# Probabilities in fp16 halves turned by DMA, row sums divided after the product with v, and another order within a slot

## What is computed

```python
h = shift_token(x); q, k, v = split(h @ wqkv)            # 8 heads of 64
q, k = rotary_xpos(l2norm(q) * qs, l2norm(k) * ksc)
attn = softmax(mask(8 * q @ k.T))                         # windows of 128 rows see 256 columns
x = x + (attn @ v) @ wo
h = layernorm(shift_token(x)) * lg + lb
a, g = split(h @ w1 + b1); x = x + (a * gelu(g)) @ w2 + b2
```

## Time and profile before

| | us |
|---|---|
| median of 3 runs (3177.46 to 3179.95) | 3179.91 |
| the profiled execution, its time | 3178.97 |
| its span, first to last instruction | 3177.2 |
| first attention and setup, to the first transfer of the slots | 774 |
| slots, two layers | 774 to 3177 |

### The profile page before, as it was taken

One profiled execution on the slowest core, in us unless ns is written; L12 is line 12 of the kernel. 1 busy time (PEld: TensorE's weight loads), 2 busy tenths in 40 slices (PEclk: granted clock), 3 DMA queues, 4 the chain that ended last, 5 costly groups with the idle time before them and its releaser, 6 DMA issues.

```text
span 3177.2 us, 79721 instructions
## 1 busy us (share of the span) xinstructions
PE 2982.5 (94%) x24952; PEld 2581.8 (81%) x24952; DVE 2656.8 (84%) x7754; ACT 1847.9 (58%) x4226; POOL 1754.4 (55%) x2083
## 2 busy tenths in 40 slices
PE   6898989783899999999999999999999999999997
PEld 3676767573688888888888888888888888888886
DVE  6878788755788888888888888899998999999895
ACT  4233241402566666666666666666676676676673
POOL 1231314024566666666666666676676676676773
PEclk9999999995899999999999999999999999999999
DMA  1120202025111111111111111222112212122221
GB/s 38 38 70 28 80 14 87 4 83 205 33 50 49 53 51 49 52 48 49 54 50 50 50 48 50 56 56 60 56 55 57 65 55 60 55 55 60 63 56 46
DMA packets 273326, 177.65 MB, mean 56 GB/s; under 512 B 95758, under 2 KB 271090, under 8 KB 272754
## 3 DMA queue, kind: packets, MB, share of 16 engines
q1 hardware_dynamic: 273138, 175.50, 19.0%
HBM read 104.08 MB, written 54.54 MB: 50 GB/s over the span
## 4 chain that ended last, share of the span: by engine, by line
PE 72%; POOL 1%; issue 1%; DVE 0%; DMA 0%; ACT 0%; POOLq 0%; SPq 0%; DVEq 0%; ACTq 0%
PE b_ps L824 17%; PE b_ps L899 14%; PE b_ps L910 10%; PE b_ps L852 8%; PE b_ps L840 7%; PE b_ps L878 6%; PE b_ps L865 6%; PE b_ps L809 2%; PE b_ps L802 2%; PE b_ps L791 1%; POOL b_sq L1145 0%; POOL b_rn L1178 0%; POOL b_t L1167 0%; POOL b_kr L1183 0%; DVE b_probs L1093 0%
## 5 line engine op out<-in xcount | busy, mean ns | idle before, releaser
L957 ACT ACTIVATE b_probs<-b_probs,b_negmax 128x256 f32<-128x256 f32 x1024 | 506.0, 496 | 78.3 <-DVE b_negmax L1093 77.5
L824 PE MATMUL b_ps<-b_wqkv,b_hT_hi 128*128 128x512 f32 x1536 | 493.0, 402 | 1.0 <-DVE b_hT_lo L981 1.0
L899 PE MATMUL b_ps<-b_h2T,b_w 128*128 128x256 f16 x4224 | 473.0, 273 | 6.5 <-DMA b_h2T<-b_xh_hl 6.4
L899 PEld LDWEIGHTS b_ps<-b_h2T,b_w 128*128 128x128 f16 x4224 | 413.6, 98 | 55.1 <-DMA b_h2T<-b_xh_hl 6.8
L1145 POOL TENSOR_TENSOR b_sq<-b_sq 128x512 f32<-128x512 f32 (+5 forms) x768 | 419.3, 546 | 62.4 <-ACT b_sq L938 22.3
L1178 POOL TENSOR_TENSOR b_rn<-b_ss_min,b_mhalf 128x16 f32<-128x16 f32 x128 | 377.2, 2947 | 108.9 <-DVE b_ss_min L1005 108.7
L1106 DVE TENSOR_SCALAR b_probs<-b_probs,b_rinv 128x256 f32<-128x256 f32 x1024 | 409.6, 442 | 18.2
L1155 POOL TENSOR_TENSOR b_rstd<-b_var,b_mhalf 128x1 f32<-128x1 f32 x128 | 72.2, 564 | 552.3 <-DVE b_var L1066 552.3
L407 PE MATMUL a_ps<-a_xn_hl,a_E 128*128 128x256 f16 x3072 | 352.5, 277 | 18.9 <-DVE a_E L290 18.9
L407 PEld LDWEIGHTS a_ps<-a_xn_hl,a_E 128*128 128x128 f16 x3072 | 303.3, 99 | 58.5 <-issue 19.9
L910 PE MATMUL b_ps<-b_w,b_hid 128*128 128x256 f32 x1536 | 342.2, 379 | 1.2 <-DVE b_hid L1129 1.2
(11 more groups left out here) (137 smaller groups left out, 6191.6 us busy)
## 6 DMA issues: line engine op xcount, KB each, us to landing
b_hx<-xs_dram SPq DMA_DIRECT2D x256, 64.0 KB, 1.9
b_rot<-rot_dram SPq DMA_DIRECT2D x128, 128.0 KB, 2.1
b_xr<-xs_dram SPq DMA_DIRECT2D x128, 128.0 KB, 2.1
xp_dram<-b_xp SPq DMA_DIRECT2D x128, 128.0 KB, 1.7
b_h<-xp_dram SPq DMA_DIRECT2D x256, 64.0 KB, 1.8
a_x_res<-in_L_attn_x_dram SPq DMA_DIRECT2D x64, 128.0 KB, 2.2
x_dram<-a_x SPq DMA_DIRECT2D x64, 128.0 KB, 1.7
xs_dram<-a_xo SPq DMA_DIRECT2D x64, 128.0 KB, 1.8
```

The costliest lines, as they stand in the source:

```text
L824: last = nc.tensor.matmul(ps[:, bank, :], hT[:, k, :], wqkv[:, ds(layer(s), 1), part, k, bank * INNER:(bank + 1) * INNER], start=(k == 0 a ...
L899: last = nc.tensor.matmul(ps[:, bank, half * 2 * P:(half + 1) * 2 * P], w1[:, ds(layer(2 * j), 1), wp, k, first:first + P], h2T[:, hp, k, ...
L957: nc.scalar.activation(probs[:, h, :], probs[:, h, :], ACT.Exp, bias=negmax[:, h:h + 1], scale=-1.0, accum_out=rowsum[:, h:h + 1]).then_in ...
```

## The change

- **Probabilities.** They stay unnormalised, with a constant `P_SHIFT` added to the exponent's bias (`shift_exponent`, four small DVE operations). ACT casts each pair of heads to an fp16 high half (`high_probs`), DVE (pairs 0, 1) and POOL (pairs 2, 3) make the low half, and SP turns each pair, 128 x 1024 fp16, into `probsT` by DMA (`turn_probs`). The 16 PE transposes of a slot, their copies out of PSUM and `normalise` go.
- **Row sums.** One reciprocal of all 8 sums; 8 fp32 products with the identity (`spread_done`, bank 3) spread it over the rows of each head; ACT copies that to `spread`; DVE multiplies it with the result of the product with v into `o_n`, from which the halves of oT are made.
- **fp16.** q, k, v come from scaled fp16 halves of hT and wqkv, v is kept as two fp16 halves (`v_hl`, made by ACT and DVE), and its product takes three fp16 passes (48 products of 128 columns). The scales come from the largest weight (setup: two reductions, an all-reduce and small steps) and, for layer 1, from the largest output of layer 0 (`layer_top` on DVE in odd slots, `batch_scales` in two slots). wqkv is loaded first in the setup.
- **b2** is a row of w2, so POOL's xb goes; ACT casts xh instead of DVE.
- **Order.** PE: q, k turned; q; k; scores; v; spread; first product chunks 0, 1 (odd slots) or half of the second product (even slots); product with v; chunks 2, 3 or the other half; hx; wo; chunks 4, 5. The feed-forward products change parity. The other engines follow, as the diff shows.

The diff, cut to its core (indentation of up to 16 blanks taken off):

```diff
-W1_BANKS = (0, 1, 6, 3, 4, 5)
+W1_BANKS = (0, 1, 6, 4, 5, 3)
+SPREAD_BANK, W2_BANK = 3, 4
+SCALE_SLOTS = (NW - 4, NW + 6)
...
+def batch_scales(nc, dve, step, before, work, top, w_scale, w_unit, h_scale, o_unit, ss_floor):
+floor, pow2, inv, root = (work[:, n:n + 1] for n in range(4))
+columns = list(h_scale.shape)
+wait(dve, step, before)
+nc.vector.tensor_scalar(floor, top, H_FLOOR, None, ALU.max).then_inc(step, 1)
+dve.wait_ge(step, before + 1)
+nc.vector.tensor_scalar(pow2.bitcast(I32), floor.bitcast(I32), 0x7F800000, None, ALU.bitwise_and).then_inc(step, 1)
+dve.wait_ge(step, before + 2)
+nc.vector.reciprocal(inv, pow2).then_inc(step, 1)
+dve.wait_ge(step, before + 3)
+nc.vector.tensor_scalar(h_scale, inv.to_broadcast(columns), H_TOP, None, ALU.mult).then_inc(step, 1)
+nc.vector.tensor_scalar(root, inv, H_TOP * NORM_FLOOR, w_scale, ALU.mult, ALU.mult).then_inc(step, 1)
+dve.wait_ge(step, before + 5)
+nc.vector.tensor_tensor(ss_floor, root.to_broadcast(columns), root.to_broadcast(columns), ALU.mult).then_inc(step, 1)
+nc.vector.tensor_scalar(o_unit, pow2.to_broadcast(columns), 1.0 / (H_TOP * V_SCALE), w_unit, ALU.mult, ALU.mult).then_inc(step, 1)
...
+sp.dma_start(wqkv_f[:].rearrange("p l k n -> p (l k) n"), w["wqkv"].rearrange("l (k p) n -> p (l k) n", p=P)).then_inc(loaded_qkv, 16)
...
+dve.wait_ge(loaded_qkv, 16)
+for l in range(LAYERS):
+    nc.vector.tensor_reduce(top_q[:, l:l + 1], wqkv_f[:, l].rearrange("p k n -> p (k n)"), AX.X, ALU.max, apply_absolute_value=True).then_inc(top_q_ready, 1)
+dve.wait_ge(top_q_shared, 1)
...
-v = sb("v", [P, 4, INNER])
+hT_hi, hT_lo = sb("hT_hi", [P, KD, P], F16), sb("hT_lo", [P, KD, P], F16)
+v_hl = sb("v_hl", [P, SLOTS, 2, INNER], F16)
...
+    def turn_probs(p):
+        t = s - 1
+        if in_range(t):
+            if p < 2:
+                wait_apart(sp, p_lo_dve, 2 * t + p + 1, passed_sp)
+            else:
+                wait_apart(sp, p_lo_pool, 2 * t + p - 1, passed_sp)
+            wait_apart(sp, pv_done, t, passed_sp)
+            sp.dma_start_transpose(probsT[:, p], probs_hl[:, p].rearrange("p a n -> p (a n)")).then_inc(pT_loaded[p], 16)
...
+    turn_probs(0)
+    turn_probs(1)
     t = s - 2
     if in_range(t):
         n = stream_block(t)
         sp.wait_ge(xp_ready, t + 1)
-        sp.dma_start(xp_v[:, ds(n, 1), :], xp[:, r % 2, :]).then_inc(xp_stored, 16)
+        sp.dma_start(xp_v[:, ds(n, 1), :], xp[:, (r - 2) % SLOTS, :]).then_inc(xp_stored, 16)
+    turn_probs(2)
+    turn_probs(3)
+    if in_range(t):
         wait_apart(sp, xp_stored, 16 * (t + 1), passed_sp)
         wait_apart(sp, xh_ready, t - 1, passed_sp)
         wait(sp, h2_loaded, 32 * t)
         sp.dma_start(h2[:, r % 2, 0:HALF], xp_v[:, ds(n, 1), 0:HALF]).then_inc(h2_loaded, 16)
         sp.dma_start(h2[:, r % 2, HALF:D], xp_prev[:, ds(n - 1, 1), HALF:D]).then_inc(h2_loaded, 16)
+    t = s - 3
+    if in_range(t):
+        wait_apart(sp, xh_lo, t + 1, passed_sp)
+        wait_apart(sp, w1_done, HC * (pairs - 2 if r % 2 == 1 else pairs - 3), passed_sp)
+        wait_apart(sp, h2T_loaded, 16 * t, passed_sp)
+        n, pair = (r - 3) % 2, (r - 3) // 2 % 2
+        sp.dma_start_transpose(h2T[:, pair, :, :, n * P:(n + 1) * P].rearrange("p a k n -> p (a k) n"),
+                               xh_hl[:].rearrange("p a d -> p (a d)")).then_inc(h2T_loaded, 16)
...
+    wait(pe, o_ready, t - 2)
...
-        pe.wait_ge(v_kept, t + 1)
         wait(pe, xp_ready, s - 2)
+        if not in_range(s - 3):
+            pe.wait_ge(v_lo, s)
         for p in range(HP):
             last = nc.tensor.transpose(ps[:, 2, p * P:(p + 1) * P], qr[:, p * P:(p + 1) * P], ident_f[:])
         last.then_inc(qT_done, 1)
         pe.wait_ge(kr_ready, t + 1)
         wait(pe, scores_kept, HEADS * t)
-        if r % 2 == 1:
-            wait(pe, hid_ready, HC * (pairs - 2) + W1_BANKS.index(6) + 1)
+        if r % 2 == 0:
+            wait(pe, hid_ready, HC * (pairs - 3) + W1_BANKS.index(6) + 1)
...
+        wait(pe, q_terms, 3 * s)
         if r % 2 == 0:
-            wait(pe, xpp_ready, s - 4)
-        else:
-            wait(pe, hid_ready, HC * (pairs - 1))
-        for p in range(HP):
-            if p == HP - 1 and in_range(s - 1):
-                pe.wait_ge(kT_lo, s)
-            pe.wait_ge(probs_ready, HEADS * t + 2 * p + 2)
-            for n in range(4):
-                last = nc.tensor.transpose(ps[:, 3 + p, n * P:(n + 1) * P],
-                                           probs[:, 2 * p + n // 2, (n % 2) * P:(n % 2 + 1) * P], ident_f[:])
-            last.then_inc(pT_done, 1)
-        pe.wait_ge(v_kept, t + 1)
-        if not in_range(s):
-            pe.wait_ge(oT_lo, t)
-        for p in range(HP):
-            pe.wait_ge(pT_kept, HP * t + p + 1)
-            for c in range(2):
-                window = (r - 2 - (r + c) % 2) % 4
-                for h in range(2):
-                    last = nc.tensor.matmul(ps[h * DH:(h + 1) * DH, 7, p * P:(p + 1) * P],
-                                            v[:, window, (2 * p + h) * DH:(2 * p + h + 1) * DH],
-                                            probsT[:, p, (2 * h + c) * P:(2 * h + c + 1) * P],
-                                            start=(c == 0), stop=(c == 1))
-        last.then_inc(pv_done, 1)
+            wait(pe, hid_ready, HC * (pairs - 3) + 1)
+        qkv(0, q_done)
+        wait(pe, k_terms, 3 * s)
+        if r % 2 == 0:
+            wait(pe, hid_ready, HC * (pairs - 3) + 2)
...
+        if r % 2 == 1:
+            wait(pe, xpp_ready, s - 5)
+        else:
+            wait(pe, hid_ready, HC * (pairs - 2))
...
+    if in_range(s):
+        wait(pe, qT_lo, s)
+        qkv(2, v_done)
     t = s - 2
+    if in_range(t):
+        pe.wait_ge(rinv_ready, t + 1)
+        if in_range(s - 1):
+            pe.wait_ge(scores_kept, HEADS * (s - 1) + BANK_READ[SPREAD_BANK])
+        elif r % 2 == 0:
+            pe.wait_ge(hid_ready, HC * (pairs - 2))
+        for p in range(HP):
+            for h, rows in enumerate(half_rows):
+                last = nc.tensor.matmul(ps[rows, SPREAD_BANK, p * P:(p + 1) * P], rinv[:, 2 * p + h:2 * p + h + 1].to_broadcast([P, DH]),
+                                        ident_f[:], start=True, stop=True)
+        last.then_inc(spread_done, 1)
+    first_product((0, 1))
+    second_product(0)
+    if in_range(t):
+        pe.wait_ge(v_lo, t + 1)
+        if not in_range(s):
+            pe.wait_ge(o_ready, t)
+        for p in range(HP):
+            pe.wait_ge(pT_loaded[p], 16 * (t + 1))
+            for c in range(2):
+                window = (r - 2 - (r + c) % 2) % 4
+                for a, (vp, pp) in enumerate(PARTS):
+                    for h in range(2):
+                        last = nc.tensor.matmul(ps[h * DH:(h + 1) * DH, 7, p * P:(p + 1) * P],
+                                                v_hl[:, window, vp, (2 * p + h) * DH:(2 * p + h + 1) * DH],
+                                                probsT[:, p, 4 * pp + 2 * h + c, :],
+                                                start=(c == 0 and a == 0), stop=(c == 1 and a == 2))
+        last.then_inc(pv_done, 1)
...
+    first_product((2, 3))
+    second_product(1)
+    if in_range(s + 1):
+        transpose_hx(s + 1, r + 1)
...
+    first_product((4, 5))
...
+    def exp_pair(p):
+        t = s - 1
+        if in_range(t):
+            if p == 0:
+                wait(act, rinv_ready, t)
+            act.wait_ge(shift_done, HP * t + p + 1)
+            for h in range(2 * p, 2 * p + 2):
+                nc.scalar.activation(probs[:, h, :], probs[:, h, :], ACT.Exp, bias=negmax[:, h:h + 1], scale=-1.0,
+                                     accum_out=rowsum[:, h:h + 1]).then_inc(exp_done, 1)
+    def high_probs(p):
+        t = s - 1
+        if in_range(t):
+            act.wait_ge(exp_done, HEADS * t + 2 * p + 2)
+            wait(act, pT_loaded[p], 16 * t)
+            nc.scalar.copy(probs_hl[:, p, 0, :], probs[:, 2 * p:2 * p + 2, :].rearrange("p h n -> p (h n)")).then_inc(p_hi, 1)
...
+    exp_pair(0)
+    if in_range(s):
         act.wait_ge(v_done, s + 1)
         wait(act, pv_done, s - 2)
-        nc.scalar.copy(v[:, r, :], ps[:, 2, :]).then_inc(v_kept, 1)
+        nc.scalar.activation(v_hl[:, r, 0, :], ps[:, 2, :], ACT.Copy, scale=V_SCALE).then_inc(v_hi, 1)
+    exp_pair(1)
     t = s - 2
     if in_range(t):
-        wait(act, pv_done, t)
-        for p in range(HP):
-            act.wait_ge(pT_done, HP * t + p + 1)
-            nc.scalar.copy(probsT[:, p, :], ps[:, 3 + p, :]).then_inc(pT_kept, 1)
-        act.wait_ge(pv_done, t + 1)
+        act.wait_ge(spread_done, t + 1)
+        wait(act, o_ready, t)
+        nc.scalar.copy(spread[:], by_pair(ps[:, SPREAD_BANK, :])).then_inc(spread_kept, 1)
+    high_probs(0)
+    if in_range(t):
+        act.wait_ge(o_ready, t + 1)
         wait(act, wo_done, t)
-        nc.scalar.copy(oT[:, 0], by_pair(ps[:, 7, :])).then_inc(oT_hi, 1)
-    t = s - 1
-    if in_range(t):
-        for p in range(HP):
```

(66 more changed lines are left out.)

331 lines of the change are left out of this document (175 added, 156 removed).

## The result

The changed kernel takes 3755.38 us (median of 4 runs, 3748.59 to 3756.22), the kernel before 3179.28 on the same chip: ratio 1.181, interval 1.179 to 1.183. It is slower by 576 us, where 286 were forecast, and lies 115 us above the range. The span is 3754.0 us, the mean granted clock 0.918 (0.976 before).

The account below looks back on a forecast made before the run. PE bounds the kernel before; after the change, PE held up by chains through ACT and DVE: pair 34.7 + 6.45 = 41.1 us, +4.5. 3179 + 276 + 10 (setup) = 3465 us, range 3300 to 3640.

Parts of the forecast that it names:

- The paths: Queues of ACT and DVE after the product with v make PE wait in four places, 6.45 us a pair.
- Turning of q behind xp: After an even slot, the next slot's turning of q waits for DVE's xp (bank 2); PE stands 2.7 us.
- Turning of k behind the hidden chunks: After an odd slot, k's turning waits for the third hidden chunk, scores start late; PE stands 2.4 us.
- Spreading behind the masking: Spread products wait until DVE has masked three heads: 0.95 us in one slot, 0.4 us in the other.
- PE's own work: PE's products and turnings without waits: 0.94 us less a slot, 34.7 us a pair.
- the lower end: Product with v if halves of the array overlap: 28 ns a product, 1.33 us; the forecast took the middle, 2.0.
- The spreading: New on PE: 8 fp32 products spreading the reciprocals, 0.95 us more a slot.
- the clock falls: Rival: a tenth of the pair at 1.2 GHz, +4 us a pair, 3700 us; chance 0.06.
- The sum: Work 34.7 plus waits 6.45 gives 41.1 us a pair, +4.5 on before; times 61, +276 us.
- the setup: Reductions, all-reduce, small operations and wqkv's earlier load before the slots: 0 to 25 us more, taken as 10.
- The transposes by DMA: On SP: 2.1 us to issue each, 3.3 to land; hidden behind PE's slot and waits, so costing nothing.
- PE stays without gaps: Rival: ACT's and DVE's queues short enough, pair 34.7 us, 3075 us; chance 0.15.

Follow-up runs that it names:

- The moves against the first and against both: Changed kernel with xp right after xh on DVE, 3593.3 us; with two exponentials and a cast ahead of oT's copy on ACT, 3583.8; together 3576.8.
- spreading behind: Against the kernel with the loop's edge moved (3350.0 us): spread products behind the product with v, second layer's output norm behind the last hidden chunk; 3347.3 us.
- other banks: Changed kernel with the xp and exponential moves, plus k turned in bank 7, q in bank 6 in odd slots, hT halves made earlier; 3616.9 us.
- gelus cut: Against the kernel with other banks: gelus and hidden chunks 2 on moved behind the next slot's copies of q and k; 3587.5 us, ratio 1.128.

## Why the prediction was right and wrong

- **The paths** (right). Turning of q behind xp in the odd slot: 2.7 us forecast, 2.8 measured, and 0.4 in the even slot, which the forecast did not have. Turning of k behind the hidden chunks: 2.4, where the scores were to follow; measured 2.7 and 0.5 at the scores. Spreading behind the masking: 1.35 against 0.8. Together 6.45 against 7.4 us a pair. The moves against the first and against both took 162 and 172 us off, together 179. That the sizes fit is in part luck: the wait for k and the wait at the scores were one wait of 2.4 in the forecast, and are two of 3.2 together.
- **PE's own work** (right in sum). 34.7 forecast; the kernel with spreading behind has the full clock in this stretch (columns as above). Its pair lasts 37.6 us there, so PE works 554 / 600 x 37.6 = 34.7.

```profile
1250.00:1850.00 600.00, 553.53 (x5533) 424.93 (x5534) 517.84 (x1470) 431.71 (x1054) 432.74 (x456) 1.00 0.48 105
```

The sum is right by luck, for its terms are not. The product with v is at the lower end, 1.48 us instead of 2.0, 31 ns a product, as the rule on packing gave (the Trainium skill, "TensorE: Matmul & The Clock Gate", part on packing small matmuls). The spreading took 0.88 us here instead of 0.95 (1.09 in the changed kernel, where it starts behind a wait). These two make a pair 1.1 us shorter, and the other products, priced as in a row without any gap, are 1.0 us longer: q, k, v take 224 ns each instead of 216, the second feed-forward product 224 a record instead of 216, the turning of k 1.1 us instead of 0.88, the rest a few ns each.
- **The clock** (the step that failed). The forecast's sum has no term for it. The rival "the clock falls" priced it at 4 us a pair, and got a chance of 0.06 on the ground that "PE would stand 2.7 us at most at a time". Measured: 38.0 - 34.7 = 3.3 us a pair, and 3.1 by the records of the granted clock. That is a tenth of PE's work at half the clock, just the condition that the rival set. The earlier trace rows showed the lower clock before the change, and the single wait in the kernel before shows 1.8 us for 3.0 of waiting. The rival wasn't another way it could go but a part of the forecast's own way: the waits it took for sure are what brings the clock down, as filling them with unread products and putting one into the kernel before both show.
- **The sum.** 8.9 us a pair instead of 4.5: waits 0.95 more, clock 3.3 more. Times 61 that is 259 of the 290 us that were missing; the rest lies in the first slots, at the change of layer and in the setup (the first load of the slots is at 786.0 instead of 774.4 us, 11.6 for the 10 forecast).
- **The transposes by DMA** (right that they cost nothing, wrong in price). Issuing one of 128x1024 takes SP 1.24 us, not 2.1, and they land 3.3 us after their start, as forecast. Doubled, they show.
- **"PE stays without gaps"** (0.15). Even with all the moves PE waits 3.8 us a pair, and the kernel stays 5% above the one before.

## What to carry to other kernels

If a forecast says that PE will stand for two or three microseconds again and again, the lower clock belongs into its sum and not among the rivals: here it added 45% to the waits themselves. That share is no constant: it was 60% for the one wait of 3.0 us, 24% for two of 2.3, and about 12% in the last kernel, whose waits are mostly about 1 us. A tightly ordered kernel has its next wait right behind the one that is taken away: look at the whole list of PE's waits before and after a move, for three of the moves here (other banks, gelus cut, spreading behind) brought little or nothing. Work taken off PE did not pay in this kernel, because ACT's and DVE's queues between two products had become longer than PE's work there, which the shares of busy time do not tell.

## What was not expected of the hardware

- One wait of PE of 3.0 us a pair costs more clock than two of 2.3: 1.8 us against 1.1. All 42 waits of the first kind (2.4 to 4.4 us) had the lower clock behind them, and only 20 of the 82 of the second, 6 of its 18 waits over 3 us not among them. PE then ran at 1.2 GHz for 3 to 4 us in most cases.
- At the edge of the loop DVE stands once a turn, for 2.7 to 3.3 us in the changed kernel and 2.1 to 4.2 with the gelus cut. The kernel before shows 1.2 to 1.5 us, in its second layer alone. A body of eight slots makes PE stand instead, up to 3.6 us.
- Some of DVE's short operations on SBUF alone last until an operation of POOL ends: 0.90 us instead of 0.15 for two columns. It happens in the two-operand form (81 of 351) and in the three-operand one (88 of 349). The Trainium skill ("GPSIMD Engine Reference", specifications) says that the two engines share their SBUF interfaces and names two cases in which they contend: a DVE operation in a 2-port mode or one with two inputs in SBUF; the two forms that were held up here would be these two.
- Two fp16 products with weights of 64 columns, sent to different halves of the array, take 31 ns each.
- A transpose by DMA of 128x1024 is issued in the time of one of 128x512, 1.24 against 1.22 us.
